# Quantised cross attention: probabilities turned as pairs of bytes, cast apart on GpSimd, and scores of two heads issued alternately

## The reference, cut to what matters

```python
q = _fq_sym(q, axis=-1); k = _fq_sym(k, axis=-1); v = _fq_sym(v, axis=2)
attn = jnp.einsum('bhqd,bhkd->bhqk', q, k)
attn = jax.nn.softmax(attn.astype(jnp.float32), axis=-1)
attn = _fq_unsigned(attn, axis=-1)
out = jnp.einsum('bhqk,bhkd->bhqd', attn, v)
return out @ Wp + bp
```

## Time and profile before

| | us |
|---|---|
| median of 3 runs | 3039.45 (3037.06 to 3040.23) |
| profiled execution, device time | 3038.51 |
| span of the profiled execution | 3036.7 |
| first eviction of the units (L1682), from the span's start | 1655.9 |
| last eviction starts | 2450.5 |

### The profile page before, as it was taken

The page is one execution under the profiler, slowest core; times in us unless marked ns, Lnnn a source line. Parts: engine busy times, 40 slices in busy tenths (PEclk is TensorE's granted clock), DMA queues, the critical chain, the costliest instruction groups (busy, mean ns, idle before and its releaser), DMA issues. The chain is left out here.

```text
span 3036.7 us, 50228 instructions
## 1 busy us (share of the span) xinstructions
PE 2498.7 (82%) x16570; PEld 1358.9 (45%) x16570; DVE 1932.5 (64%) x3686; ACT 1482.0 (49%) x2055; POOL 409.3 (13%) x454
## 2 busy tenths in 40 slices
PE   6874775999979999999664888787878865999998
PEld 3333554555547777777552222222222232444444
DVE  6995556667743333333456998888888845666665
ACT  5552332444433333333232776666666633666664
POOL 0001220111012222333133000000000001001100
PEclk9886776999979999999776555555555567999999
DMA  2000000000010000000000999999999940000001
GB/s 83 0 0 19 0 0 12 16 26 21 21 29 18 18 17 17 17 17 9 21 0 18 177 176 169 165 169 162 171 163 171 173 71 17 24 23 16 23 23 36
DMA packets 594876, 175.35 MB, mean 58 GB/s; under 512 B 548642, under 2 KB 594212, under 8 KB 594724
## 3 DMA queue, kind: packets, MB, share of 16 engines
q1 hardware_dynamic: 594724, 173.44, 29.6%
HBM read 37.07 MB, written 2.10 MB: 13 GB/s over the span
## 5 line engine op out<-in xcount | busy, mean ns | idle before, releaser
L1682 DVE TENSOR_SCALAR_CACHE_REDUCE ctxT<-psum,e_nsq 128x1024 f32<-128x1024 f32 x512 | 637.2, 1282 | 74.2 <-issue 54.1
L1651 PE MATMUL psum<-e_KT,e_Qs 48*128 48x512 bf16 x1024 | 519.9, 611 | 181.7 <-DVE ctxT L1682 151.0
L1703 ACT ACTIVATE xh<-ctxT,e_ebias 128x2048 uint16<-128x2048 f32 x128 | 256.2, 2002 | 134.0 <-DVE e_ebias L1686 134.0
L1703 ACT ACTIVATE xl<-ctxT,e_ebias 128x2048 uint16<-128x2048 f32 x128 | 256.2, 2002 | 119.2 <-DVE e_ebias L1686 119.2
L1651 PEld LDWEIGHTS psum<-e_KT,e_Qs 48*128 48x128 bf16 x1024 | 67.3, 104 | 415.8 <-issue 408.1
L103 PE MATMUL psum<-xh,d_WT 128*128 128x512 f16 x768 | 229.4, 381 | 2.6 <-DVE d_WT L1214 2.6
L1662 PEld LDWEIGHTS psum<-e_Vi,xnT 128*128 128x128 f16 x4096 | 129.5, 105 | 216.8 <-issue 216.8
L1233 DVE TENSOR_TENSOR d_ACC<-psum,d_ACC 128x512 f32<-128x512 f32 x128 | 82.5, 686 | 171.1 <-PE psum L1287 171.1
L103 PE MATMUL psum<-xh,f_WA 128*128 128x512 f16 x544 | 152.7, 383 | 13.9 <-DVEq L1896 11.8
L103 PE MATMUL psum<-xh,c_Wx 128*128 128x512 f16 x576 | 161.3, 383 | 0.8 <-DVE X L960 0.8
L1662 PE MATMUL psum<-e_Vi,xnT 128*128 128x16 f16 x4096 | 152.5, 175 | 8.1 <-DMA xnT<-xh 4.5
(11 more groups left out here) (312 smaller groups left out, 4965.9 us busy)
## 6 DMA issues: line engine op xcount, KB each, us to landing
d_Wn<-in_L_attn_w_qkv SPq DMA_DIRECT2D x16, 384.0 KB, 3.2
f_W<-in_L_ffn_w_routed SPq DMA_DIRECT2D x32, 176.0 KB, 2.5
ctx_rows<-in_ctx SPq DMA_DIRECT2D x1, 2048.0 KB, 8.6
X<-in_x SPq DMA_DIRECT2D x1, 2048.0 KB, 14.0
c_Wgu<-in_L_ffn_rg SPq DMA_DIRECT2D x16, 128.0 KB, 2.1
c_Wgu<-in_L_ffn_rw SPq DMA_DIRECT2D x16, 128.0 KB, 2.2
c_Wd<-in_L_ffn_rw SPq DMA_DIRECT2D x16, 128.0 KB, 2.2
d_Wn<-in_L_attn_w_gate SPq DMA_DIRECT2D x16, 128.0 KB, 3.0
```

The costliest lines, as they stand in the source:

```text
L1651: mm = pe.matmul(m.bank[b + q], Qs[rows, x.u // 2 % QSLOTS, :], KTt[rows, j // 2, (2 * hf + q) * BLK:(2 * hf + q + 1) * BLK], start=True, ...
L1682: dve.tensor_scalar(S32[:, sl, hf * HALF:(hf + 1) * HALF].rearrange("p (a b) -> p a b", a=2), m.psum[:, b:b + 2, :], nsq[:, ds(x.n(), 1)], ...
L1703: act.activation(e16[x.u % SLOTS], S32[:, x.u % 2, :], ACT.Exp, bias=ebias[:, x.u % 2:x.u % 2 + 1], scale=-1.0, accum_out=esum[:, ds(x.n() ...
```

## The change

The probabilities are rounded to bytes instead of 16-bit integers. The DMA turns pairs of bytes as two-byte values, 128 x 1024 per unit instead of 128 x 2048. A new GpSimd instruction casts the bytes to bf16 and puts the even and the odd ones apart, into two blocks of 128 columns; for that the keys in KT are interleaved by tile (L1466), so that V stays in its order. The bias for the exponential moves from VectorE to GpSimd. The scores of the two heads of a pair are issued together: for each 512 columns a matmul on rows 0 to 47 and then one on rows 64 to 111; both halves of keys so produce two chunks (one for each head), and VectorE evicts four chunks for each pair of units, with four slots for evicted scores instead of two. The product with V comes seven units behind the scores, and the cast three units behind.

```diff
-        Vi = sb("Vi", [P, KT, H, HD], F16)
+        Vi = sb("Vi", [P, KT, H, HD], BF16)
...
-                            act.activation(KTt[:, :, ds(t * P, P)], m.bank[b + 1].bitcast(BF16)
-                                           .rearrange("p (a b) -> p a b", a=PR), ACT.Copy).then_inc(stored, 1)
+                            act.activation(KTt[:, :, ds(i * 2 * TPB * P + tt // 2 * 2 * P, 2 * P)]
+                                           .rearrange("p a (q b) -> p a q b", b=2)[:, :, :, tt % 2],
+                                           m.bank[b + 1].bitcast(BF16).rearrange("p (a b) -> p a b", a=PR),
+                                           ACT.Copy).then_inc(stored, 1)
...
-        BODY, SLOTS, LAG, QAHEAD, QSLOTS = 48, 4, 6, 3, 6
+        BODY, SLOTS, LAG, LATE, QAHEAD, QSLOTS = 48, 4, 7, 3, 4, 6
...
-                        m.wait_apart(pool, scored, (pair - (QSLOTS - 1)) * 4)
+                        m.wait_apart(pool, scored, (pair - (QSLOTS - 1)) * 2)
...
                 def step(x):
-                    if not x.exists():
-                        return
                     ahead = x.back(-2 * QAHEAD)
                     if x.u % 2 == 0 and ahead.exists():
                         fetch(ahead)
+                    if x.exists():
+                        m.wait_apart(pool, score_out, x.n(2, 4) + 3 + x.u % 2)
+                        sl = x.u % SLOTS
+                        pool.tensor_scalar(ebias[:, sl:sl + 1], mn[:, sl, 0:1], mn[:, sl, 1:2], LN255,
+                                           ALU.min, ALU.add).then_inc(biased, 1)
+                    if x.back(LATE).exists():
+                        unpack(x.back(LATE))
+
+                def unpack(x):
+                    m.wait_apart(pool, laid[x.u % SLOTS], x.n(SLOTS, 16) + 16)
+                    if x.at_least(SLOTS):
+                        m.wait_apart(pool, mixed, x.n() - (SLOTS - 1))
+                    pool.tensor_copy(PT[:, x.u % SLOTS, :, :].rearrange("p (c b) q -> p c q b", b=2),
+                                     P8[:, x.u % SLOTS, :, :].rearrange("p c q -> p (c q)").bitcast(U8)
+                                     .rearrange("p (c q b) -> p c q b", c=KT // 2, b=2)).then_inc(unpacked, 1)
...
                     if x.at_least(SLOTS):
-                        m.wait_apart(sp, mixed, x.n() - (SLOTS - 1))
-                    sp.dma_start_transpose(PT[:, x.u % SLOTS, :, :], e16[x.u % SLOTS].bitcast(F16)).then_inc(laid[x.u % SLOTS], 16)
+                        m.wait_apart(sp, unpacked, x.n() - (SLOTS - 1))
+                    sp.dma_start_transpose(P8[:, x.u % SLOTS, :, :], e8[:, x.u % SLOTS, :].bitcast(U16)).then_inc(laid[x.u % SLOTS], 16)
...
                     for hf in range(2):
+                        c = 2 * x.u + 2 * hf
                         if x.at_least(2):
-                            m.wait_apart(pe, score_out, x.n(1, 2) + hf - 2)
+                            m.wait_apart(pe, score_out, x.n(1, 2) + 2 * hf - 1)
...
                         for q in range(2):
-                            mm = pe.matmul(m.bank[b + q], Qs[rows, x.u // 2 % QSLOTS, :],
-                                           KTt[rows, j // 2, (2 * hf + q) * BLK:(2 * hf + q + 1) * BLK],
-                                           start=True, stop=True)
+                            col = (2 * hf + q) * BLK
+                            for odd in range(2):
+                                rows = slice(64 * odd, 64 * odd + 48)
+                                mm = pe.matmul(m.bank[pair_banks(c + odd) + q], Qs[rows, x.u // 2 % QSLOTS, :],
+                                               KTt[rows, x.j // 2, col:col + BLK], start=True, stop=True)
                         mm.then_inc(scored, 1)
...
-                    m.wait_apart(pe, laid[x.u % SLOTS], x.n(SLOTS, 16) + 16)
+                    m.wait_apart(pe, unpacked, x.n() + 1)
...
-                    if x.exists():
+                    if x.u % 2 == 0 and x.exists():
                         score(x)
...
-                    if x.at_least(2):
-                        m.wait_apart(dve, exped, x.n() - 1)
+                    if x.u % 2:
+                        return
+                    if x.at_least(SLOTS):
+                        m.wait_apart(dve, exped, x.n() - (SLOTS - 2))
                     for hf in range(2):
...
+                        m.wait_apart(dve, scored, x.n() + hf + 1)
+                        for odd in range(2):
+                            sl = (x.u + odd) % SLOTS
+                            b = pair_banks(2 * x.u + 2 * hf + odd)
+                            dve.tensor_scalar(S32[sl][:, hf * HALF:(hf + 1) * HALF].rearrange("p (a b) -> p a b", a=2),
+                                              m.psum[:, b:b + 2, :], nsq[:, ds(x.n() + odd, 1)], None, ALU.mult, ALU.min,
+                                              accum_out=mn[:, sl, hf:hf + 1]).then_inc(score_out, 1)
...
-                    m.wait_apart(dve, score_out, x.n(1, 2) + 2)
-                    dve.tensor_scalar(ebias[:, sl:sl + 1], mn[:, sl, 0:1], mn[:, sl, 1:2], LN255,
-                                      ALU.min, ALU.add).then_inc(biased, 1)
...
-                        act.activation(e16[x.u % SLOTS], S32[:, x.u % 2, :], ACT.Exp, bias=ebias[:, x.u % 2:x.u % 2 + 1],
+                        act.activation(e8[:, x.u % SLOTS, :], S32[x.u % SLOTS], ACT.Exp, bias=ebias[:, x.u % SLOTS:x.u % SLOTS + 1],
```

More of the change, by code:

```diff
@@ L1375, in quantised_attention @@
     chain_s, vmaxed, vall = (m.sem(f"e_{n}") for n in ("chain", "vmax", "vall"))
-    q_here, scored, score_out, biased, exped, mixed, normed, chain2 = (m.sem(f"e_{n}") for n in (
-        "q_here", "scored", "score_out", "biased", "exped", "mixed", "normed", "chain2"))
+    q_here, scored, score_out, biased, exped, unpacked, mixed, normed, chain2 = (m.sem(f"e_{n}") for n in (
+        "q_here", "scored", "score_out", "biased", "exped", "unpacked", "mixed", "normed", "chain2"))
     laid = [m.sem(f"e_laid{i}") for i in range(4)]
@@ L1556, in quantised_attention @@
         N = NT * H
-        BODY, SLOTS, LAG, QAHEAD, QSLOTS = 48, 4, 6, 3, 6
+        BODY, SLOTS, LAG, LATE, QAHEAD, QSLOTS = 48, 4, 7, 3, 4, 6
         Qs = sb("Qs", [P, QSLOTS, P], BF16)
-        mn = sb("mn", [P, 2, 2])
-        ebias = sb("ebias", [P, 2])
+        mn = sb("mn", [P, SLOTS, 2])
+        ebias = sb("ebias", [P, SLOTS])
         esum = sb("esum", [P, N])
         Osb = sb("Osb", [P, NT, D])
[L1565 to L1568, removed]
+        Smore = sb("Smore", [P, 2, TOK])
+        S32 = [m.ctxT[:, 0, :], m.ctxT[:, 1, :], Smore[:, 0, :], Smore[:, 1, :]]
+        PT = m.xnT[:, :, :].rearrange("p a b -> p (a b)").bitcast(BF16).rearrange("p (s k q) -> p s k q", s=SLOTS, k=KT)
+        e8 = m.xh[:, :, :].rearrange("p a b -> p (a b)").bitcast(U8).rearrange("p (s k) -> p s k", s=SLOTS)
+        P8 = m.xl[:, :, :].rearrange("p a b -> p (a b)").bitcast(U16).rearrange("p (s c q) -> p s c q", s=SLOTS, c=KT // 2)
         class Unit:
@@ L1622, in step @@
                         fetch(ahead)
+                    if x.exists():
[12 more added lines that the diff above has]
+                                     .rearrange("p (c q b) -> p c q b", c=KT // 2, b=2)).then_inc(unpacked, 1)
                 for p in range(QAHEAD):
                     fetch(Unit(0, 2 * p))
-                loop(pool, step)
+                loop(pool, step, LATE)
             @block.sync
@@ L1639, in score @@
                 def score(x):
[L1640 to L1643, removed]
+                    m.wait_apart(pe, q_here, x.n(2) + 1)
                     for hf in range(2):
+                        c = 2 * x.u + 2 * hf
                         if x.at_least(2):
-                            m.wait_apart(pe, score_out, x.n(1, 2) + hf - 2)
-                        elif 2 * x.u + hf >= 3:
-                            pe.wait_ge(score_out, 2 * x.u + hf - 2)
-                        b = pair_banks(2 * x.u + hf)
+                            m.wait_apart(pe, score_out, x.n(1, 2) + 2 * hf - 1)
+                        elif c + 1 >= 3:
+                            pe.wait_ge(score_out, c - 1)
                         for q in range(2):
-                            mm = pe.matmul(m.bank[b + q], Qs[rows, x.u // 2 % QSLOTS, :],
-                                           KTt[rows, j // 2, (2 * hf + q) * BLK:(2 * hf + q + 1) * BLK],
-                                           start=True, stop=True)
+                            col = (2 * hf + q) * BLK
[3 more added lines that the diff above has]
+                                               KTt[rows, x.j // 2, col:col + BLK], start=True, stop=True)
                         mm.then_inc(scored, 1)
@@ L1675, in step @@
                 def step(x):
-                    sl = x.u % 2
-                    if x.at_least(2):
-                        m.wait_apart(dve, exped, x.n() - 1)
+                    if x.u % 2:
+                        return
+                    if x.at_least(SLOTS):
```

(8 more changed lines are left out.)

## The result

The changed kernel takes 4733.64 us (median of 4 runs, 4732.17 to 4733.82) where the kernel before took 3038.26 in the same runs: a ratio of 1.558, 95% interval 1.555 to 1.561. The forecast was 2964 us, in a range of 2870 to 3200. The loss of 1695 us lies in the one stage that was changed, and in one instruction of it.

The account below looks back on a forecast made before the run. VectorE was taken as the bound, 2.93 us a unit written out and 3.09 looped. Gains 64 x (2.93 - 2.65) = 18 and 192 x (3.09 - 2.78) = 59.5, less 3, took 74.5 off 3038.5: 2964 us, range 2870 to 3200.

Parts of the forecast that it names:

- the lower end, 1.89: GpSimd's cast of 2048 elements: 1.89 us, from a straight line through copies and a cast written in runs.
- The upper end: GpSimd's cast, estimated from above by a slow copy or a two-input operation: 4.1 to 4.7 us.
- Rival 1: GpSimd becomes the bound through its cast; slower, 3463 us at a 4.1 us cast; chance 0.26.
- (2U + 1.2) / 2: GpSimd's time per unit, U being the cast: takes over from about U = 2.1, gain gone at 2.5.
- The rest of the sum: Attention stage apart from the cast: bank cycle of 2.65 us a unit written out, 2.78 in the loop.
- The stalls at the body's ends: Four stalls at ends of the attention loop's body, 3.67 us each, expected to stay.
- the line through the earlier trace: GpSimd copies and a cast written in runs, 0.83 ns an element plus 0.19 us, giving 1.89 us.
- My ground for the exponential: ScalarE's exponential stays at 2.0 us with bytes as result, since K's copy to a narrower type kept its rate.
- T: TensorE's time for a batch of four score matmuls on two row halves: 1.05 us.
- rival 2: TensorE's row halves don't overlap in this order: four score matmuls take 1.86 us, total 3171 us; chance 0.05.
- Rival 3: DMA transposes of byte pairs take no less time, 2.97 us a unit: 3018 to 3040 us; chance 0.09.
- close behind: The DMA, at a share of 0.96 in mid-stage, was taken as nearly as binding as VectorE.

Follow-up runs that it names:

- read_apart: The changed kernel with the cast's two innermost loops exchanged, so bytes are read in steps of 2 and written straight: 2947.77 us, ratio 0.970.
- one_half: The changed kernel with a straight cast and V-product weights loaded in steps, both heads' score matmuls on rows 0 to 47: 3157.75 us, ratio 1.039.
- Bytes_alone: The kernel before with only the byte probabilities and a repaired GpSimd cast, scores and bias as before: 3040.90 us, ratio 1.0008.
- scores_alone: The changed kernel with 16-bit probabilities and no cast, keeping paired scores, four slots and the bias on GpSimd: 2947.79 us, ratio 0.970.
- unpaired_16: The changed kernel with 16-bit probabilities, no cast, and scores unit by unit waiting for one pair of banks: 2947.33 us, ratio 0.970.

## Why the prediction was wrong

*The step that failed* is "I take the lower end, 1.89". The cast's rows below were all of instructions that write straight or in runs, and the only feature of this cast that no row had, writing in turn to two places 256 bytes apart, was the one with the price. I named it, and weighed it as unlikely, because I put the slowness of the one slow copy down to what ran beside it. The upper end was no bound either: 4.1 to 4.7 us came from a copy beside VectorE and from a two-input operation, neither of which says anything of scattered writes. So the range of 2870 to 3200 was built on two ends that both missed the quantity, which was 9.22.

*Rival 1 was right in its mechanism.* GpSimd became the bound, from the place I gave, and its formula (2U + 1.2) / 2 gives 9.8 for U = 9.22, where 9.72 was measured; of the 1.2 it was 1.0. Put into the sum with before's 795.9 / 256 = 3.11, (9.72 - 3.11) x 256 is 1692 us, where 1695 was measured. It got a chance of 0.26 with a price of 3463 us, when 4734 was due.

*The Trainium skill was nearer than my rows, and I gave it no weight in the sum.* Its "GPSIMD Engine Reference", section 7, says that reads in steps of over 8 bytes cost about half as much again. It says nothing of writes, and no run here reads in such steps. The runs show that writes have a price of their own, and a harsher one: less the 0.19 us of an instruction, it is 1.1 ns an element at 4 bytes and 2.2 at 8, against 0.83 straight, and 4.4 ns at 256 bytes in turn. The estimate that I made from the page, 4.9 us, was still half of the 9.20. The same page's best case of 1.8 cycles an element (section 3.1) is not the rate of plain casts and copies here: 1.89 us for 2048 elements, less the 0.19, is 1.0 cycle, and that agrees with the 1.03 cycles that the same section gives for the shortest loop bodies.

*The rest of the sum held.* With the cast repaired the time is 2948 against the 2964 that I forecast. A pair takes 5.30 us written out, as reckoned (2 x 2.65), and 5.38 in the loop, where I had 5.56: the loop costs 0.08, once for a pair (0.23 of idle at its end, 0.15 in its middle), where I had 0.13 twice; why the middle of a pair shows none is open. That is 96 x 0.18 = 17 us, nearly all of the 16 between 2964 and 2948. The stalls at the body's ends did not stay as they were: three of 4.9 to 5.1 us came in place of four of 3.67, nearly the same sum by luck. The straight cast is 1.89, as the line through the earlier trace rows said. The DMA lands in 3.0 us instead of 4.3, and its share in read_apart is 0.58 from 1800 to 2300 us, forecast 0.55, though I had counted the packets too high: halving took 262,144 off 594,724, so a unit had 2048 and not 2,300. My ground for the exponential, the copy of K "to a narrower type", was misread, since that row copies bf16 to bf16; with bytes as its result the exponential still takes 2002 ns. T is 1.04, forecast 1.05, and one_half took 3158 us, where rival 2 had reckoned 3171.

*Rival 3 and the DMA's share.* I took a share of 0.96 as "close behind". Bytes_alone shows no gain from halving the traffic at that pace, and scores_alone that the queue gives 191 GB/s, 14% more than 168. But the concern was right one step further on: in unpaired_16 191 GB/s is the end of it, and only there do the bytes pay, 59 us (2947.33 against 2888.13).

## What to carry to other kernels

Ask of every operation on GpSimd where it writes: let the output run straight and put the step on the input, since the same permutation cost 1.89 us one way and 9.20 the other, with the type of no account. The input's step here was 2 bytes; longer ones were not run. When no row of the profile shows a pattern that the change brings, its price is open upwards, however well the size and the type are covered, and a range has to say so, or the pattern has to be avoided. And when one bound is relieved, look at how many buffers the next hand-over waits for at once: waiting for one pair of banks instead of two made the pairing of heads superfluous, once the DMA had room (2888 us without it, 2948 with it).

## What the runs showed of the hardware that I had not expected

- GpSimd's writes: for 2048 elements 1.89 us straight, 2.45 at 4 bytes apart, 4.71 at 8, 5.84 at 10, 9.20 in turn to two places 256 bytes apart; pairs of neighbours with gaps of 4 bytes 1.89.
- VectorE, writing the same 2048 bytes as bf16 in the same alternating pattern, takes 5.31 us, where a straight copy of 2048 f32 elements took it 1.23. Its masks and shifts of 512 32-bit words take 0.43 us each, which would be another way to take the bytes apart; it wasn't tried.
- TensorE starts matmuls of a free row half ahead of earlier ones that wait for their own half: four in 1.04 us in either order of issue, two of them within 0.01 us of each other.
- Weights loaded in steps of two elements cost the same 105 ns as straight ones.
- A query copy on GpSimd that follows a slow cast shows 0.52 us instead of 0.29, as its record begins before the cast's ends (3017.28 against 3008.46 + 9.23 = 3017.69 in the timeline above).
- Transposes of 128 x 2048 two-byte values went no faster than one in 2.73 us (191 GB/s) in unpaired_16, with a DMA share of 1.15; at 168 GB/s and 0.96 they held nothing up.
